# Latent attention and expert layer on one core: TensorE's attention program unrolled, one softmax division moved to the next window, three more units written back to PSUM

## The chip, the cores and the metric

The kernel runs on one core of a Trainium2 chip. The metric is device time in microseconds of one execution. The engines of the core work side by side and meet at semaphores: TensorE (PE) multiplies matrices and writes PSUM, VectorE (DVE) and ScalarE (ACT) work elementwise, GpSimd (POOL) too but without PSUM, and SyncE (SP) issues DMAs, each after the one before it in its program.

## What is computed

Two layers, each added to its input. The first is attention of 1024 tokens of 256 numbers (4 batches, 16 heads of 64) over 1024 + 128 keys, of which 77 come from the context and the rest of that tile is masked. The second is a mixture of 8 experts with a shared one. Only the attention matters for the change:

```python
    qn = rmsnorm(q, qn_g) * scale
    kn = rmsnorm(k, kn_g)
    sim = jnp.einsum('bhid,bhjd->bhij', qn, kn)
    sim = jnp.where(padded_mask[:, None, None, :], sim, max_neg)
    attn = jax.nn.softmax(sim.astype(jnp.float32), axis=-1).astype(sim.dtype)
    out = jnp.einsum('bhij,bhjd->bhid', attn, v)
```

All matrix products are taken in about float32 accuracy by splitting each factor into an upper and a lower part and multiplying three of the four combinations.

## The kernel before

The attention runs as 32 **windows**. A window is one pair of heads of one batch: `Window(v, s)`, with `s` 0 or 1 and `v` from 0 to 15, so that `w = 2 v + s` counts from 0 to 31. Windows with even w and the odd one behind it form a *pair* here; a preparation pass stands ahead of the first (`v = -1`). Every engine runs the same list of windows, its own part of each.

A window has 18 **units** d = 0 to 17. Units 0 to 8 go through the nine key tiles for the first 512 queries of both heads (half 0), units 9 to 17 for the last 512 (half 1). Unit d goes through the engines like this:

- PE `scores(w, d)`, line 972: six products of keys and queries into the bank pair `ps_s[d % 2]`.
- ACT, lines 828 and 829: the exponential once into `pr_hi` (rounded, upper part) and once in full, to `full_of(d)`. For the units in `SPARED` (0, 1, 9, 16, 17) that is the SBUF tile `pr[d % 2]`; for the others the scores in `ps_s` are overwritten with it.
- DVE, line 718: `pr_lo = full - pr_hi`, the lower part, called lo(d) below. It raises `s_lo`.
- PE `values_half` for unit d, line 1008: the first half of the value products is issued in unit d + 2 (`first`), the second in unit d + 3 (`second`), into `ps_o`.

The scores of unit d + 2 go into the bank pair that unit d used. PE therefore waits ahead of `scores(d + 2)` for `s_exp` of unit d (ACT's reading is over) where d is in `SPARED`, and for `s_lo` of unit d (DVE's reading is over too) where it isn't. In the units 2, 4, 6, 8, 11, 13 and 15 PE has further work: it turns keys and queries of the next window (line 902) and projects those of the window after (lines 925, 938). The units 16, 17, 0 and 1 have none.

The value products carry a 65th row, the sum of the exponentials. When the nine tiles of a half are done, DVE copies `ps_o` to `o_sb[h]` (`output`, line 649; in unit 10 for half 0, in unit 1 of the next window for half 1), and PE may not start the next half's values, `first(11)` and `first(2)`, before that copy (`s_o`). The softmax's division is then a chain of its own for each half, which SP drives:

1. `spread` (lines 305, 307): the row of sums goes to HBM and comes back as 128 x 8.
2. DVE `invert`, line 678: reciprocals.
3. `broadcast` (lines 313, 315): the reciprocals go to HBM (4 KB, "put") and come back copied to 64 partitions, 256 KB, into the **one** tile `rec`.
4. DVE `divide`, line 683: `o_sb[h] = o_sb[h] * rec`.
5. `store` (line 321): 256 KB of `o_sb[h]` to HBM.

Half 0 (tile `o_first`) is copied in unit 10, inverted in unit 13 and divided in unit 16 of its own window; half 1 (`o_second`) is copied in unit 1, inverted in unit 5 and divided in unit 9 of the next window. Since `rec` is one tile, half 1 may be broadcast only when the division of half 0 is over.

POOL squares and normalises the projections of the next window (lines 458, 460, 462); DVE sums its squares in units 14, 17 and 2 (`squares`, lines 691 and 693).

`windows()` writes windows 0 and 1 and the last two out, and runs the 28 between them as a loop of 14 rounds, one pair a round, on PE, ACT, DVE and POOL; SP has a similar loop. Each engine's program holds two versions of the attention, behind a test of the input gains (`either`): with running maxima (`general`) and without. The inputs take the one without.

Of the kernel before, what the change touches and what calls it, by code (L numbers as in the profile page):

```python
# [26 lines left out]
WINDOWS = HEADS // 2  # L27
# [51 lines left out]
PROJECTED = {6: (0,), 8: (1, 2), 11: (3, 4), 13: (5, 6), 15: (7, 8)}  # L79
HALVED = (8, 13, 15)  # L80
BETWEEN = (2, 11)
SPARED = (0, 1, 9, 16, 17)
JOBS = TURNS + KT
PREP = [(c, g) for g in range(2) for c in range(C)] + [(c, None) for c in range(C)]
PREPS = len(PREP)
# [70 lines left out]
def attention(nc, carry, Wout, x, ctx_in, mask, ln_x_g, ln_x_b, ln_l_g, ln_l_b, qn_g, kn_g, lnT, Wq, Wkv, maskRow, maskCol, attT, rden, routed, out, Wfc_s, Wfc, w1S, o_second):  # L156

    with ExitStack() as ctx:
# [121 lines left out]
        def _(sp):  # L280
# [20 lines left out]
            def spread(w, g, before):  # L301

                half = w.n(2, g - 2 * before)
                wait_then(s_o, w.n(2, g + 1 - 2 * before))
                sp.dma_start(rden[bass.ds(half, 1)].unsqueeze(0), o_sb[g][DH:DH + 1, :].unsqueeze(1)).then_inc(s_put, 16)
                wait_then(s_put, w.n(64, 32 * g + 16 - 64 * before))
                sp.dma_start(den[:, g, :], rden[bass.ds(half, 1)].rearrange("h (p k) -> p (h k)", p=P)).then_inc(s_den, 16)
# [11 lines left out]
            def store(w, g, before):  # L319
                wait_then(s_norm, w.n(2, g - 2 * before + 1))  # L320
                sp.dma_start(pair_v[g][bass.ds(w.n(1, -before), 1)].rearrange("w d r n -> d (w r) n"),
                             o_sb[g][0:DH, :].rearrange("d (r n) -> d r n", r=2)).then_inc(s_store[g], 16)
# [26 lines left out]
            def window(w):  # L349
# [15 lines left out]
                    load_mask(mask_b, w.other)  # L365
                if w.attend and not w.first:
                    spread(w, 1, 1)
                    broadcast(w, 1, 1)
                if w.proj and not (opening and w.s == 0):
                    wait_then(s_wlo, w.n(1, 3))  # L370
# [3 lines left out]
                if w.attend:  # L374
                    if not w.first:
                        store(w, 1, 1)
                    spread(w, 0, 0)
                    broadcast(w, 0, 0)
                    store(w, 0, 0)
                if closing(w) and w.s == 0:  # L380
                    sp.wait_ge(s_v, w.n(2, 4))
                    sp.wait_ge(s_nrm, w.n(GROUPS, 2 * GROUPS))
# [153 lines left out]
        def _(dve):  # L536
# [168 lines left out]
            def dve_windows(general):  # L705
                def window(w):
                    for d in range(UNITS):
# [12 lines left out]
                        if w.attend and not w.first:  # L720
                            if d == 5:
                                invert(w, 1, 1)
                            if d == 9:
                                divide(w, 1, 1)
                        if w.attend and d == 13:
                            invert(w, 0, 0)
                        if w.attend and d == 16:
                            divide(w, 0, 0)
                        if w.turn:
                            for i in TURNED.get(d, ()):  # L730
# [124 lines left out]
        def _(pe):  # L855
# [156 lines left out]
            def pe_windows(general):  # L1012
# [47 lines left out]
                        if isinstance(w.v, int) and w.v == -1:  # L1060
                            opening(w, d)

                windows(pe, window)
                for d in range(LAG):
                    values(Window(WINDOWS // 2, 0), d - LAG)

# [840 lines left out]
```

## Time and profile before

| | |
|---|---|
| median of 3 runs | 2600.8 us (2599.01 to 2604.87) |
| the profiled execution | 2599.23 us |
| its span, first to last instruction | 2597.4 us |
| PE busy | 2426.4 us, 93% |
| DVE busy | 1811.9 us, 70% |
| ACT busy | 1705.9 us, 66% |
| POOL busy | 1190.5 us, 46% |
| mean granted clock of TensorE | 0.982 |

The attention's windows fill the span from 93 to about 1770 us; behind them come the output projection and the experts. A busy share is an average over stages, and a busy PE is not a PE at its peak: what counts is where PE stands idle and whom it waits for.

### The profile page before, as it was taken

The page shows a single profiled execution, that of the slowest core. Times are in us where ns is not written, and L with a number is a line of the kernel's source. Part 1 is how long each engine was busy: PE and PEld are TensorE (multiplying, and loading weights), DVE is VectorE, ACT ScalarE, POOL GpSimd, SP SyncE. Part 2 cuts the span into 40 slices and gives each one's busy share as a digit, 9 for nine tenths or more (in the row PEclk, how much of TensorE's full clock was granted, in tenths as well). Part 3 has the DMA queues.
Part 4 walks back from the last instruction along what each step waited for, and adds up shares of the span by engine and source line. Part 5 has one row for each costly group of instructions (what it writes and reads, how often), then busy time and mean ns, then how long its engine had stood idle before and what let it go on. Part 6 is the DMA issues. An engine that isn't in the chain of part 4 may idle for free. (4 is left out here: it accounts for less than half of the span.)

```text
span 2597.4 us, 55511 instructions
## 1 busy us (share of the span) xinstructions
PE 2426.4 (93%) x20310; PEld 2014.8 (78%) x20310; DVE 1811.9 (70%) x2452; ACT 1705.9 (66%) x2286; POOL 1190.5 (46%) x783
## 2 busy tenths in 40 slices
PE   4799999999999999999999999997989999999998
PEld 3677677777776777777777777665989999999997
DVE  7667767677667766776667766775876566767775
ACT  2677777888887887777778777783333334444453
POOL 4334433444334433443344433442533526666665
PEclk8899999999999999999999999998999999999999
DMA  6322332233223332233223322246732459999996
GB/s 196 138 81 81 117 107 79 87 115 107 87 79 113 100 96 86 83 118 104 79 87 115 107 87 79 86 119 129 165 92 72 139 176 321 322 319 318 325 321 173
DMA packets 231564, 363.77 MB, mean 140 GB/s; under 512 B 59559, under 2 KB 139739, under 8 KB 227400
## 3 DMA queue, kind: packets, MB, share of 16 engines
q1 hardware_dynamic: 204694, 301.66, 37.7%
q0 software_dynamic: 25696, 58.82, 8.0%
q8 instruction: 164, 2.69, 0.4%
q10 hardware_dynamic: 978, 0.34, 0.1%
q14 instruction: 32, 0.26, 0.0%
HBM read 280.90 MB, written 79.85 MB: 139 GB/s over the span
## 5 line engine op out<-in xcount | busy, mean ns | idle before, releaser
L718 DVE TENSOR_TENSOR pr_lo<-ps_s,pr_hi 128x1024 fp32r<-128x1024 f32 x416 | 505.0, 1220 | 287.0 <-ACT ps_s L829 287.0
L828 ACT ACTIVATE pr_hi<-ps_s 128x1024 fp32r<-128x1024 f32 x512 | 526.2, 1028 | 231.9 <-PE ps_s L972 160.8
L1008 PE MATMUL ps_o<-pr_hi,vA 64*65 64x512 f32 x2292 | 489.7, 399 | 52.5 <-DVE pr_lo L718 31.6
L1008 PE MATMUL ps_o<-pr_lo,vA 64*65 64x512 f32 x2292 | 483.0, 392 | 0.0
L1008 PE MATMUL ps_o<-pr_hi,vC 64*65 64x512 f32 x2292 | 482.1, 391 | 0.0
L460 POOL TENSOR_TENSOR rs<-ss,minus_half 128x16 f32<-128x16 f32 (+1 forms) x96 | 225.7, 2351 | 480.8 <-DVE ss L693 480.8
L1666 ACT ACTIVATE ht<-f_ps_h,b 128x256 f32<-128x256 f32 x440 | 184.6, 471 | 341.6 <-PE f_ps_h L1598 341.6
L829 ACT ACTIVATE ps_s<-ps_s 128x1024 f32<-128x1024 f32 x384 | 392.5, 1022 | 0.0
L458 POOL TENSOR_TENSOR sq<-raw 128x1024 f32<-128x1024 f32 (+1 forms) x96 | 166.2, 1731 | 436.9 <-ACT raw L773 436.9
L1598 PE MATMUL f_ps_h<-xT_hi,w 128*128 128x256 f32 x1760 | 355.4, 285 | 3.6 <-DVE xT_lo L1700 3.1
L718 DVE TENSOR_TENSOR pr_lo<-pr,pr_hi 128x1024 fp32r<-128x1024 f32 x160 | 241.0, 1508 | 159.1 <-ACT pr L829 154.5
L1611 PE MATMUL f_ps_y<-w,h_hi 128*128 128x256 f32 x1760 | 325.8, 283 | 0.0
L1598 PEld LDWEIGHTS f_ps_h<-xT_hi,w 128*128 128x128 f32 x1760 | 288.2, 190 | 4.5 <-DVE xT_lo L1700 3.9
L1008 PEld LDWEIGHTS ps_o<-pr_hi,vA 64*65 64x65 f32 x2292 | 179.8, 133 | 137.9 <-issue 53.3
L1525 POOL TENSOR_TENSOR w<-w2raw,w 128x1024 fp32r<-128x1024 f32 x80 | 206.3, 2580 | 171.9 <-ACT w L1652 168.5
L1611 PEld LDWEIGHTS f_ps_y<-w,h_hi 128*128 128x128 f32 x1760 | 272.4, 190 | 0.0
L972 PE MATMUL ps_s<-q_hi,k_hi 64*128 64x512 f32 x1152 | 241.4, 398 | 28.7 <-issue 20.9
L1611 PE MATMUL f_ps_y<-w,h_lo 128*128 128x256 f32 x880 | 249.0, 283 | 0.0
L1598 PE MATMUL f_ps_h<-xT_lo,w 128*128 128x256 f32 x880 | 248.9, 283 | 0.0
L1008 PEld LDWEIGHTS ps_o<-pr_lo,vA 64*65 64x65 f32 x2292 | 179.0, 133 | 88.7 <-issue 1.6
L938 PE MATMUL ps_m<-w_sb,lnT_sb 64*128 64x384 f32 (+1 forms) x2304 | 241.0, 329 | 3.6 <-DVE k_lo L658 2.5
L972 PE MATMUL ps_s<-q_hi,k_lo 64*128 64x512 f32 x1152 | 238.6, 392 | 0.0
(220 smaller groups left out, 4611.8 us busy)
## 6 DMA issues: line engine op xcount, KB each, us to landing
w<-w1S_dram SPq DMA_DIRECT2D x160, 512.0 KB, 6.0
lnT_sb<-lnT_dram SPq DMA_DIRECT2D x31, 2304.0 KB, 9.6
w2raw<-in_L_ffn_Wproj SPq DMA_DIRECT2D x78, 512.0 KB, 6.8
w1S_dram<-cut POOLq DMA_DIRECT2D x36, 512.0 KB, 3.0
rec<-rden_dram SPq DMA_DIRECT2D x63, 256.0 KB, 3.8
routed_dram<-empty POOLq DMA_DIRECT2D x28, 387.0 KB, 3.6
xt<-routed_dram SPq DMA_DIRECT2D x39, 258.0 KB, 6.6
w_raw<-in_L_xattn_Wkv SPq DMA_DIRECT2D x66, 128.0 KB, 4.0
```

Source lines behind the costliest of these rows:

```text
L458: g.tensor_tensor(sq[:, 0:n_, j0 * DH:], qk, qk, ALU.mult).then_inc(s_sq, 1)
L460: g.tensor_tensor(rs[:, 0:sums], ss[:, 0:sums], minus_half[:, 0:sums], ALU.pow).then_inc(s_pool, 1)
L718: v.tensor_tensor(pr_lo[:, ring(w, d), :], full_of(d), pr_hi[:, ring(w, d), :].bitcast(F32), ALU.subtract).then_inc(s_lo, 1)
L828: act.activation(pr_hi[:, ring(w, d), :], ps_s[:, d % 2, :], ACT.Exp, bias=bias)
L829: act.activation(full_of(d), ps_s[:, d % 2, :], ACT.Exp, bias=bias).then_inc(s_exp, 1)
L938: ins = mm(ps_m[:, tile % 2, lo:3 * PW], lnT_sb[rows, a, c, tile * P:(tile + 1) * P], w_sb[rows, w.slot, b, c, lo:], start=part == 0 and k ...
L972: ins = mm(ps_s[:, d % 2, 512 * h:512 * h + 512], key[rows, w.slot, keys], x[rows, w.slot, cols], start=not general and i == 0, stop=i == 2)
L1008: ins = mm(ps_o[0:DH + 1, h, :], v_[rows, h], p_[rows, 512 * h:512 * h + 512], start=k == 0 and part == 0 and i == 0, stop=k == KT - 1 and ...
L1525: nc.gpsimd.tensor_tensor(w2[:, slot, 2 * h:2 * h + 2, 1], w2raw[:, slot, 2 * h:2 * h + 2], w2[:, slot, 2 * h:2 * h + 2, 0].bitcast(F32), ...
L1598: ins = mm(ps_h[:, p % 2, i, :], w1[:, slot, p, k, lo, i, :], x_[:, parity, k, :], start=k_ == 0, stop=k_ == 3 * C - 1)
L1611: ins = mm(ps_y[:, parity, r, 0:D], h[:, parity, c, r * P:(r + 1) * P], w2[:, slot, p, lo, c % 2, :], start=c == 0 and k_ == 0, stop=c == ...
L1666: ins = act.activation(ht[:, p, i, :], ps_h[:, p % 2, i, :], ACT.Gelu_apprx_tanh, bias=b1[:, slot, p, i:i + 1])
```

## The change

It has three parts, all in the attention.

- TensorE's program for the version without maxima is no longer a loop: all 32 windows are written out. The other engines keep their loops.
- The division of half 0 moves from unit 16 of its window to unit 7 of the next one, two units ahead of the division of half 1; its store moves with it, on SP between the spread and the broadcast of half 1. The last window keeps its division in unit 16.
- `SPARED` shrinks to the units 1 and 9: units 0, 16 and 17 write the full exponential over the scores in PSUM like the others. DVE then reads it from PSUM, and PE waits for DVE, not for ACT alone, ahead of `scores(0)`, `scores(1)` and `scores(2)`.

```diff
-SPARED = (0, 1, 9, 16, 17)
+SPARED = (1, 9)
...
                 if w.attend and not w.first:
                     spread(w, 1, 1)
+                    store(w, 0, 1)
                     broadcast(w, 1, 1)
...
                     spread(w, 0, 0)
                     broadcast(w, 0, 0)
-                    store(w, 0, 0)
+                    if closing(w) and w.s == 1:
+                        store(w, 0, 0)
...
                             if d == 5:
                                 invert(w, 1, 1)
-                            if d == 9:
-                                divide(w, 1, 1)
+                            if d in (7, 9):
+                                divide(w, (d - 7) // 2, 1)
                         if w.attend and d == 13:
                             invert(w, 0, 0)
-                        if w.attend and d == 16:
+                        if closing(w) and w.s == 1 and d == 16:
                             divide(w, 0, 0)
...
-                windows(pe, window)
+                if general:
+                    windows(pe, window)
+                else:
+                    for v in range(-1, WINDOWS // 2):
+                        for s in range(2):
+                            window(Window(v, s))
```

VectorE from unit 16 of window 0 to unit 1 of window 1 (the same stands between any two windows); line 718 is lo(d), lines 691 and 693 are `squares`, line 649 the copy of half 1. Before:

```order
L718 TENSOR_TENSOR pr_lo<-pr,pr_hi 128x1024
L683 TENSOR_TENSOR o_first<-o_first,rec 64x1024
L718 TENSOR_TENSOR pr_lo<-pr,pr_hi 128x1024
L691 TENSOR_REDUCE ss<-sq 128x16
L693 TENSOR_SCALAR ss<-ss 128x16
L718 TENSOR_TENSOR pr_lo<-pr,pr_hi 128x1024
L649 COPY o_second<-ps_o 65x1024
L718 TENSOR_TENSOR pr_lo<-pr,pr_hi 128x1024
```

The same place now, from unit 15 on, where line numbers are two higher:

```order
L720 TENSOR_TENSOR pr_lo<-ps_s,pr_hi 128x1024 x3
L693 TENSOR_REDUCE ss<-sq 128x16
L695 TENSOR_SCALAR ss<-ss 128x16
L720 TENSOR_TENSOR pr_lo<-ps_s,pr_hi 128x1024
L651 COPY o_second<-ps_o 65x1024
L720 TENSOR_TENSOR pr_lo<-pr,pr_hi 128x1024
```

The division of `o_first` is gone from between lo(16) and lo(17), and lo(16), lo(17) and lo(0) read `ps_s`.

VectorE in units 7 to 10 of window 1, before:

```order
L718 TENSOR_TENSOR pr_lo<-ps_s,pr_hi 128x1024 x2
L718 TENSOR_TENSOR pr_lo<-pr,pr_hi 128x1024
L683 TENSOR_TENSOR o_second<-o_second,rec 64x1024
L649 COPY o_first<-ps_o 65x1024
L718 TENSOR_TENSOR pr_lo<-ps_s,pr_hi 128x1024 x4
```

And now:

```order
L720 TENSOR_TENSOR pr_lo<-ps_s,pr_hi 128x1024
L685 TENSOR_TENSOR o_first<-o_first,rec 64x1024
L720 TENSOR_TENSOR pr_lo<-ps_s,pr_hi 128x1024
L720 TENSOR_TENSOR pr_lo<-pr,pr_hi 128x1024
L685 TENSOR_TENSOR o_second<-o_second,rec 64x1024
L651 COPY o_first<-ps_o 65x1024
L720 TENSOR_TENSOR pr_lo<-ps_s,pr_hi 128x1024 x4
```

The division of `o_first` has come in between lo(7) and lo(8); the rest is unmoved.

SyncE in window 28, from the spread of half 1 on. Before:

```order
L305 DMA rden_dram<-o_second 1x1024
L307 DMA den<-rden_dram 128x8
L313 DMA rden_dram<-den 128x8
L315 DMA rec<-rden_dram 64x1024
L290 DMA w_raw<-in_L_xattn_Wq 128x2x128
L290 DMA w_raw<-in_L_xattn_Wkv 128x2x128 x2
L321 DMA attT_dram<-o_second 64x2x512
```

And now:

```order
L305 DMA rden_dram<-o_second 1x1024
L307 DMA den<-rden_dram 128x8
L321 DMA attT_dram<-o_first 64x2x512
L313 DMA rden_dram<-den 128x8
L315 DMA rec<-rden_dram 64x1024
L290 DMA w_raw<-in_L_xattn_Wq 128x2x128
L290 DMA w_raw<-in_L_xattn_Wkv 128x2x128 x2
L321 DMA attT_dram<-o_second 64x2x512
```

The store of `o_first`, with its wait for the division, now stands ahead of the put and of the load of `rec` for half 1.

## Rows read from the trace of the kernel before

**Rows 1.** Waits of all engines, over the span: us in total, times, longest us

```profile
PE ps_o L1008 <- DVE pr_lo L718: 31.6, 18, 3.4
...
PE ps_s L972 <- issue: 20.9, 10, 2.3
...
PE ps_o L1008 <- DVE o_second L649: 16.8, 31, 1.5
```

**Rows 2.** Timeline of PE, window 16 into 17: start us, us, operation, [idle before <-releaser]

```profile
986.45 0.40 PE L972 MATMUL ps_s<-q_hi,k_hi 64*128 64x512 f32 x2
...
996.04 0.45 PE L1008 MATMUL ps_o<-pr_hi,vA 64*65 64x512 f32 x2 [1.66 <-DVE pr_lo L718]
...
1000.53 0.43 PE L972 MATMUL ps_s<-q_hi,k_hi 64*128 64x512 f32 x2
```

**Rows 3.** Timeline of PE, window 17 into 18, where a round ends

```profile
1038.92 0.41 PE L972 MATMUL ps_s<-q_hi,k_hi 64*128 64x512 f32 x2
...
1045.53 0.50 PE L972 MATMUL ps_s<-q_hi,k_hi 64*128 64x512 f32 x2 [2.29 <-issue]
...
1049.78 0.42 PE L972 MATMUL ps_s<-q_hi,k_hi 64*128 64x512 f32 x2
...
1053.55 0.43 PE L972 MATMUL ps_s<-q_hi,k_hi 64*128 64x512 f32 x2
```

**Rows 4.** Timeline of DVE at the same place

```profile
1041.81 2.68 DVE L718 TENSOR_TENSOR pr_lo<-pr,pr_hi 128x1024 fp32r<-128x1024 f32 x1 [2.24 <-ACT pr L829]
1044.42 2.91 DVE L683 TENSOR_TENSOR o_first<-o_first,rec 64x1024 f32<-64x1024 f32 x1
...
1048.39 1.20 DVE L691 TENSOR_REDUCE ss<-sq 128x16 f32<-128x1024 f32 x1
...
1050.15 1.22 DVE L718 TENSOR_TENSOR pr_lo<-pr,pr_hi 128x1024 fp32r<-128x1024 f32 x1 [0.35 <-issue]
```

**Rows 5.** Timeline of POOL, the squaring alone and beside DVE's division

```profile
1025.69 1.89 POOL L458 TENSOR_TENSOR sq<-raw 128x1024 f32<-128x1024 f32 x1 [13.78 <-ACT raw L773]
...
1043.37 2.88 POOL L458 TENSOR_TENSOR sq<-raw 128x1024 f32<-128x1024 f32 x1
```

**Rows 6.** Timeline of ACT, the second exponential of unit 17

```profile
1042.92 1.10 ACT L829 ACTIVATE pr<-ps_s,mcol 128x1024 f32<-128x1024 f32 x1
```

**Rows 7.** Timeline of DVE, units 7 to 11 of window 17

```profile
1014.67 1.23 DVE L718 TENSOR_TENSOR pr_lo<-ps_s,pr_hi 128x1024 fp32r<-128x1024 f32 x1 [1.97 <-ACT ps_s L829]
...
1020.93 1.23 DVE L718 TENSOR_TENSOR pr_lo<-pr,pr_hi 128x1024 fp32r<-128x1024 f32 x1 [2.82 <-ACT pr L829]
1022.07 1.21 DVE L683 TENSOR_TENSOR o_second<-o_second,rec 64x1024 f32<-64x1024 f32 x1
1023.88 1.22 DVE L649 COPY o_first<-ps_o 65x1024 f32<-65x1024 f32 x1 [0.59 <-PE ps_o L1008]
```

**Rows 8.** Timeline of PE, units 7 to 12 of window 17

```profile
1011.80 0.40 PE L972 MATMUL ps_s<-q_hi,k_hi 64*128 64x512 f32 x2
...
1025.98 0.44 PE L1008 MATMUL ps_o<-pr_hi,vA 64*65 64x512 f32 x2
...
1026.72 0.39 PE L972 MATMUL ps_s<-q_hi,k_hi 64*128 64x512 f32 x2
```

**Rows 9.** Timeline of SP's queue, window 17: start us, us of issuing

```profile
1010.30 0.36 SPq L313 DMA_DIRECT2D rden_dram<-den  x1
1011.86 0.54 SPq L315 DMA_DIRECT2D rec<-rden_dram  x1
...
1023.54 0.69 SPq L321 DMA_DIRECT2D attT_dram<-o_second  x1
```

**Rows 10.** Waits of SP's queue, over the span

```profile
SPq L299 <- DMA rden_dram<-o_second: 130.8, 31, 6.2
```

**Rows 11.** Line 315, the load of rec: from its issue to its landing

```profile
DMA to landing us min/median/max: 3.4/3.8/7.4
```

**Rows 12.** Line 321, the store of a divided half, likewise

```profile
DMA to landing us min/median/max: 3.0/3.2/3.5
```

## The prediction

> **What bounds the kernel now.** I read the waits of all engines first. In the attention PE leads and stands idle in few places: 31.6 us in 18 pieces ahead of value products, for a lower part from DVE, 20.9 us in 10 pieces ahead of scores for nothing but "issue", and 16.8 us in 31 pieces for the copy of half 1 [rows 1]. The reader is to see that the counts are those of window boundaries. Then I read PE's timeline over two boundaries. Into an odd window it waits 1.66 us for lo(17), and scores(3) starts 14.08 us after the old window's scores(16) (1000.53 - 986.45) [rows 2]. Into an even window inside the loop it stands 2.29 us with nobody to wait for, and the same stretch takes 14.63 us [rows 3]. That is where PE's round ends, 13 times. Boundaries without such a jump are 18: the 16 into odd windows, and those into windows 2 and 30.
>
> DVE's timeline tells why lo(17) is late [rows 4]: lo(16) takes 2.68 us and the division behind it 2.91, where lo from PSUM takes 1.23 and the same division 1.21 [rows 7]. POOL's squaring, beside that division, takes 2.88 instead of 1.89 [rows 5]. DVE instructions that read two SBUF tiles and POOL's work stretch each other; lo from PSUM doesn't suffer. By the Trainium skill ("SBUF — State Buffer", "Who interferes with whom") the two engines share one pair of ports under an exclusive lock; the durations agree.
>
> **The change, the boundary.** Times from scores(16) = 0, which is 1038.92 [rows 3]. A unit without further work takes PE 2.07: (1049.78 - 1045.53) / 2, less 0.05, since the first product after a halt takes 0.50 and not 0.41 and costs 0.1 once [rows 3].
> - *The jump* goes with the loop. Alone it would be worth little: where PE doesn't jump it waits for lo(17) instead, so 14.63 would become 14.08.
> - *lo(16)* starts at 2.89 as now [rows 4] and ends at 4.12, for it reads PSUM. scores(0) would go at 4.14: no wait to speak of, though it now waits for DVE.
> - *lo(17)*: ACT's second exponential ends at 5.10 (1042.92 + 1.10) [rows 6], with no division ahead of it lo(17) ends at 6.36. scores(1), due at 6.24, goes at 6.41 (0.05 for the wake-up).
> - *lo(0)* stands behind `squares`. POOL's squaring starts at 4.45 and, undisturbed, ends 1.89 later at 6.34 [rows 5]; the sums start at 6.42. From them to lo(0) it is 1.76 now (1048.39 to 1050.15), 0.35 of it idle at DVE's own jump [rows 4]: 1.41 where DVE doesn't jump. lo(0) runs from 7.83 to 9.06, scores(2) goes at 9.11 instead of 8.58. This 0.5 is the price of taking unit 0 out of `SPARED`; the cover that unit 0 had is gone.
> - From scores(2) to scores(3) it is 3.77 as now (1049.78 to 1053.55) [rows 3], the short wait for the copy of half 1 in it; with 0.1 for the restart, scores(3) goes at 12.98.
>
> So 14.08 becomes 12.98, 1.10 less, 18 times; and 14.63 becomes 13.33, since DVE still jumps (0.35), 1.30 less, 13 times. **Gain: 19.8 + 16.9 = 37 us.** ACT's own jump is not seen in the trace; hi(0) has 0.7 before lo(0) would feel it, so I take nothing. From below: if scores(2) need not wait, 0.6 more a boundary, 55 us in all; if ACT and POOL are each 0.4 later, 12 less, 25 us.
>
> **The change, the middle of the window.** Times from scores(7) = 0, which is 1011.80 [rows 8]. The moved division costs DVE nothing by itself: it lies in idle time (1.97 us stand ahead of lo(7) and 2.82 ahead of lo(9) [rows 7]). But `rec` is one tile, and SP issues in order. What was over long before is now a chain:
> 1. lo(7) starts at 2.87, the next DVE instruction 1.14 later as after lo(9) (1020.93 to 1022.07) [rows 7]: the division of half 0 runs from 4.01 to 5.22.
> 2. SP issues the store 0.26 after a division's end (1023.28 to 1023.54) [rows 9]: 5.48.
> 3. The put comes behind it. A put alone lets `rec` be loaded 1.56 after its issue (1010.30 to 1011.86) [rows 9]; one with a long load ahead of it in SP's queue made SP wait 130.8 us in 31 times, 4.2 each and up to 6.2 [rows 10]. So a put is not over before what is ahead of it, and the store takes 3.2 to land [rows 12]: SP goes on at 8.7. The other bound is a put that overtakes: 5.48 + 0.69 of issuing + 1.56 = 7.7.
> 4. `rec` lands 3.8 after its issue, at least 3.4, at most 7.4 [rows 11]. I take the median: 12.5. It came long before the division until now; the division of half 1 started at 10.27 [rows 7].
> 5. DVE stands in order: division 12.5 to 13.7, then the copy of half 0, 13.65 to 14.87 (now from 12.08), then lo(10), 14.8 to 16.03.
> 6. PE: first(11), due at 14.18, waits for the copy until 14.92; scores(12), due at 14.92 [rows 8], waits for lo(10) until 16.08. With 0.1 for the restart PE loses **1.26 us a window**. lo(11) ends at 17.2, before scores(13) wants it at 18.2, so it ends there.
>
> **Cost: 31 x 1.26 = 39 us.** Its bounds: with 7.7 and 3.4 `rec` lands at 11.1 and lo(10) ends at 14.7, inside the cover, cost 0; each 0.1 us that `rec` lands after 11.4 costs 3 us in all, so landing at 13.3 costs 64. I take the store's landing and the median of the load, the rows most like the case.
>
> Here one rule of the notes speaks against the change. What the rows show is in point 3. The Trainium skill ("DMA: Bandwidth & Descriptors", "Queues, rings and completion order") says that a DMA's semaphore increment lands only after every earlier write of the same DMA engine. By that rule the put waits for the store's landing, 8.7 and 39 us; by a put that overtakes it would be 1 us less a window, 8 us in all. The 31 waits of 4.2 us bear the rule out, behind a load and not behind a store.
>
> **Other moves.** The load of the next keys (2.3 MB) no longer stands behind the division and goes out earlier; PE shows no wait for it, so it gains nothing. The `w_raw` loads stand behind the load of `rec` on SP and go 8.6 us later with it (now 1011.86 [rows 9], then 8.7 after 1011.80); they are wanted in unit 16, which starts 27.1 after scores(7) [rows 3, 8]. Writing the full exponential to PSUM I cost at nothing for ACT: it is the same instruction with another target.
>
> **The sum.** 39 - 37 = +2 us on the profiled execution's 2599.2. That execution lies 1.6 below the median of 2600.8; the difference is carried over, so 2603.
>
> **Rivals.**
> - *The put is not held up.* For it: a put's 4 KB are nothing beside the bandwidth, and the long waits of [rows 10] are behind a load ten times the store's size. Against it: the queue is one. `rec` lands at 11.1 to 12.0, cost 0 to 20, net -17 to -37: about 2573.
> - *`rec` comes later still* (the other side). Right behind it SP issues three `w_raw` loads, and POOL's loads are near; landings up to 7.4 occur [rows 11]. It decides from a landing 0.3 after my 12.5; at 4.6 after its issue, 13.3, the cost is 64 and the net +27: 2628. The last two windows, which have no projections between units 7 and 12 to cover anything, go this way as well.
> - *The written-out PE doesn't lose its idle piece*, since its instructions arrive late wherever they come from. For it: "issue" names no releaser. Against it: at the boundaries without a jump, where the code is straight or inside a round, there is no such piece [rows 2]. Then the 13 even boundaries gain nothing: net +19, 2620. The Trainium skill ("Runtime: NRT & Kernel Launch", "Instruction fetch mechanics") says that fetching ahead is sequential and a taken branch breaks it; by that rule the piece goes and this rival is out.
>
> **How the numbers follow.** My case 0.52, from 2588 to 2618 by errors of 0.4 us a window in either term; the first rival 0.22, the second 0.20, the third 0.06. A measurement tells some 0.2%, 5 us, from no change. Of my case I give 0.14 to faster by more, 0.23 to within, 0.15 to slower by more. Faster: 0.14 + 0.22 = 0.36; same 0.23; slower 0.15 + 0.20 + 0.06 = 0.41. The range leaves out the ends of the rivals: 2570 to 2629; my case alone 2588 to 2618.
>
> **What would show it.** In the changed kernel's trace: no idle "issue" piece ahead of scores; scores(16) to scores(3) near 13.0; no 2.9 us division, lo(0), lo(16) and lo(17) at 1.2 us from `ps_s`; a short wait of PE for lo(0) ahead of scores(2). In the middle: DVE idle ahead of the division of `o_second`, ended by the DMA of `rec`, 2.2 us a window; PE idle ahead of first(11) for the copy of `o_first`, 0.7, and ahead of scores(12) for lo(10), 0.4. If DVE doesn't wait for `rec`, the first rival holds; if it waits 3 us or more, the second. The prediction is wrong altogether if windows shorten at the boundary by another amount than they lengthen in the middle and neither chain is in the trace.

## The result

Over four executions each, the changed kernel takes 2626.1 us (2621.1 to 2627.5) and the kernel before 2602.2 (2599.0 to 2604.9). The ratio is 1.0089, with a 95% interval of 1.0073 to 1.0105: **0.9% slower, +24 us**. The forecast was 2603, in a range of 2570 to 2629, so the time lies inside the range, at its far end, beside the second rival (2628) and outside what the prediction gave its own case (2588 to 2618).

The waits of all engines, over the span of the changed kernel (2623.4 us): us in total, times, longest us.

```profile
DVE o_second L685 <- DMA rec<-rden_dram: 87.5, 31, 9.0
...
PE ps_o L1010 <- DVE o_first L651: 52.0, 31, 9.3
...
PE ps_s L974 <- DVE pr_lo L720: 21.7, 33, 7.7
```

"issue" is gone from PE's waits, and so are the 31.6 us for lo(17) [rows 1]. The gain at the boundary is real. In their place DVE waits for `rec` in all 31 windows that divide a half behind it, 2.8 us each on the mean, and PE for the copy of `o_first` that stands behind that division on DVE.

The same place as [rows 3], window 17 into 18, in PE's timeline (start, us, operation, idle before and what ended it):

```profile
1054.03 0.41 PE L974 MATMUL ps_s<-q_hi,k_hi 64*128 64x512 f32 x2
...
1063.47 0.50 PE L974 MATMUL ps_s<-q_hi,k_hi 64*128 64x512 f32 x2 [0.69 <-DVE pr_lo L720]
...
1067.32 0.42 PE L974 MATMUL ps_s<-q_hi,k_hi 64*128 64x512 f32 x2
```

scores(16) to scores(3) is 13.29 us (1067.32 - 1054.03), where it was 14.63. The idle piece of 2.29 us is gone, and a short wait for lo(0) stands ahead of scores(2). DVE there, against [rows 4]:

```profile
1056.92 1.23 DVE L720 TENSOR_TENSOR pr_lo<-ps_s,pr_hi 128x1024 fp32r<-128x1024 f32 x1 [2.24 <-ACT ps_s L831]
1059.14 1.22 DVE L720 TENSOR_TENSOR pr_lo<-ps_s,pr_hi 128x1024 fp32r<-128x1024 f32 x1 [0.99 <-ACT ps_s L831]
1060.41 1.22 DVE L693 TENSOR_REDUCE ss<-sq 128x16 f32<-128x1024 f32 x1
1061.67 0.18 DVE L695 TENSOR_SCALAR ss<-ss 128x16 f32<-128x16 f32 x1
1062.19 1.22 DVE L720 TENSOR_TENSOR pr_lo<-ps_s,pr_hi 128x1024 fp32r<-128x1024 f32 x1 [0.35 <-issue]
```

lo(16), 2.68 us before, takes 1.23, and no division of 2.91 stands behind it. lo(0) stands behind the sums of squares, as forecast.

The middle of window 17, whose scores(7) start at 1025.35. First SP's queue (start, us of issuing), then DVE, then PE:

```profile
1030.80 0.69 SPq L321 DMA_DIRECT2D attT_dram<-o_first  x1
1031.68 0.46 SPq L313 DMA_DIRECT2D rden_dram<-den  x1
1034.35 0.54 SPq L315 DMA_DIRECT2D rec<-rden_dram  x1
```

```profile
1029.36 1.21 DVE L685 TENSOR_TENSOR o_first<-o_first,rec 64x1024 f32<-64x1024 f32 x1
...
1038.18 1.22 DVE L685 TENSOR_TENSOR o_second<-o_second,rec 64x1024 f32<-64x1024 f32 x1 [2.48 <-DMA rec<-rden_dram]
1039.33 1.21 DVE L651 COPY o_first<-ps_o 65x1024 f32<-65x1024 f32 x1
```

```profile
1040.68 0.45 PE L1010 MATMUL ps_o<-pr_hi,vA 64*65 64x512 f32 x2 [1.09 <-DVE o_first L651]
...
1041.72 0.50 PE L974 MATMUL ps_s<-q_hi,k_hi 64*128 64x512 f32 x2
...
1043.90 0.42 PE L974 MATMUL ps_s<-q_hi,k_hi 64*128 64x512 f32 x2
```

Read it as one chain: division at +4.01, store at +5.45, put at +6.33, load of `rec` at +9.00, second division at +12.83, copy, PE's wait of 1.09. scores(7) to scores(13) takes 18.55 us, where it took 16.99 (1028.79 - 1011.80).

The records of the DMA packets show how the put is held. The store's packets (2,048 bytes each) start from 1032.2 to 1033.5, the put's 128 packets of 32 bytes from 1033.4 to 1033.7, so the put's data move only when the store's are nearly through. The last of the store's 16 completions comes at 1034.02, the last of the put's at 1034.19.

By windows, the starts of `scores` in the two traces subtracted from each other:

| us, after less before | sum | of one window |
|---|---|---|
| boundaries into windows 1 to 31 | -41.8 | -1.1 odd, -1.6 even |
| middles of windows 1 to 29, but for 5 and 10 | +41.8 | +1.55 |
| middles of windows 5 and 10 | +12.6 | +6.3 |
| middles of windows 30 and 31 | +13.2 | +10.0, +3.2 |
| window 0, up to its scores(16) | +1.8 | |
| the rest | -1.6 | |
| span | +26.0 | |

So the change wins 42 us at the boundaries, gives all of it back in the regular middles, and loses 26 more in four windows in which `rec` comes later than in the others.

**Windows 5 and 10.** DVE in window 5, whose scores(7) start at 379.80, and SP beside it:

```profile
394.35 2.30 DVE L685 TENSOR_TENSOR o_second<-o_second,rec 64x1024 f32<-64x1024 f32 x1 [4.20 <-DMA rec<-rden_dram]
```

```profile
386.12 0.46 SPq L313 DMA_DIRECT2D rden_dram<-den  x1
390.19 0.53 SPq L315 DMA_DIRECT2D rec<-rden_dram  x1
```

The put takes 4.07 us from its issue to the next DMA, not 2.67. In the records of the DMA packets 120 of its 128 small packets are over by 388.2, and 15 of its 16 completions are there by 388.60, as early as in window 17. A packet of instructions (queue 8, 16,384 bytes) starts at 388.0 and takes 0.947 us; the put's last eight packets run behind it, at 389.0, and the sixteenth completion comes at 390.04, 1.4 us late. That the eight stood behind this packet on one ring is read from the times; the records don't name the ring. The division then starts in the middle of POOL's squaring and takes 2.30, while the squaring is not stretched:

```profile
393.69 1.89 POOL L460 TENSOR_TENSOR sq<-raw 128x1024 f32<-128x1024 f32 x1 [13.63 <-ACT raw L775]
```

PE waits 3.89 instead of 1.09, and what that costs it is more than the wait. The core's work by stretch: us; busy us and instructions of PE, PEld, DVE, ACT, POOL; granted clock; DMA share; GB/s:

```profile
380.00:394.00 14.00, 14.00 (x120) 10.90 (x116) 5.55 (x6) 11.32 (x14) 0.37 (x2) 1.00 0.46 134
394.00:398.00 4.00, 0.11 (x3) 0.10 (x4) 3.65 (x3) 0.49 (x1) 1.57 (x1) 0.76 0.12 29
398.00:403.00 5.00, 5.00 (x24) 3.34 (x26) 2.28 (x3) 1.94 (x2) 0.00 (x0) 0.51 0.25 54
```

After nearly 4 us of idle time PE works for 5 us at a granted clock of 0.51, which is the lower of its two levels (1.2 of 2.4 GHz). From first(11) to scores(13) it takes 5.09 us (403.02 - 397.93), where it took 3.22 in window 17 (1043.90 - 1040.68): another 1.9 us. So the 4.7 us by which this middle is longer than that of window 17 are 1.7 of late landing, 1.1 of stretched division and 1.9 of clock.

**Window 30** has no projections in units 8 to 11, and POOL loads and stores weights there. SP's timeline and DVE's:

```profile
1718.87 0.70 SPq L313 DMA_DIRECT2D rden_dram<-den  x1
1726.02 0.50 SPq L315 DMA_DIRECT2D rec<-rden_dram  x1
```

```profile
1729.77 1.22 DVE L685 TENSOR_TENSOR o_second<-o_second,rec 64x1024 f32<-64x1024 f32 x1 [8.98 <-DMA rec<-rden_dram]
```

The put takes 7.15 us, since the store ahead of it lands only 7.65 after its issue: its packets are mixed with those of POOL's load and store. Some of it is again a packet of instructions. One starts at 1722.7; 120 of the put's packets have started by 1723.9, the last eight start at 1725.3. In e6 the load of `rec` goes at +13.7 as here (+13.6), with such a packet in nearly the same place, in e7 and e12, which have none there, at +11.8 and +11.9. PE stands idle for 9.28 us in this window, and its granted clock is 0.50 for the 5 us behind.

### The profile page after: what moved, and what is told of

It is laid out like the page before. It is cut to its first block and busy times, and to the rows that moved or that the text cites. A ratio compares the mean times of both kernels' runs of the same rounds, so it can differ in the third digit from the quotient of the medians.

```text
span 2623.4 us, 54379 instructions
## 1 busy us (share of the span) xinstructions
PE 2442.9 (93%) x20310; PEld 2018.6 (77%) x20310; DVE 1733.5 (66%) x2452; ACT 1707.0 (65%) x2286; POOL 1161.5 (44%) x783
## 5 line engine op out<-in xcount | busy, mean ns | idle before, releaser
L720 DVE TENSOR_TENSOR pr_lo<-ps_s,pr_hi 128x1024 fp32r<-128x1024 f32 x512 | 621.9, 1219 | 354.3 <-ACT ps_s L831 348.5
L831 ACT ACTIVATE ps_s<-ps_s 128x1024 f32<-128x1024 f32 x448 | 457.1, 1020 | 0.0
L462 POOL TENSOR_TENSOR rs<-ss,minus_half 128x16 f32<-128x16 f32 (+1 forms) x96 | 208.8, 2175 | 523.6 <-DVE ss L695 523.6
L974 PE MATMUL ps_s<-q_hi,k_hi 64*128 64x512 f32 x1152 | 253.2, 417 | 25.3 <-DVE pr_lo L720 21.7
L974 PE MATMUL ps_s<-q_lo,k_hi 64*128 64x512 f32 x1152 | 239.4, 392 | 0.0
```

The costliest lines, as they stand in the source:

```text
L462: g.tensor_tensor(rs[:, 0:sums], ss[:, 0:sums], minus_half[:, 0:sums], ALU.pow).then_inc(s_pool, 1)
L720: v.tensor_tensor(pr_lo[:, ring(w, d), :], full_of(d), pr_hi[:, ring(w, d), :].bitcast(F32), ALU.subtract).then_inc(s_lo, 1)
L831: act.activation(full_of(d), ps_s[:, d % 2, :], ACT.Exp, bias=bias).then_inc(s_exp, 1)
L974: ins = mm(ps_s[:, d % 2, 512 * h:512 * h + 512], key[rows, w.slot, keys], x[rows, w.slot, cols], start=not general and i == 0, stop=i == 2)
```

## The experiments

Theory: the boundary gains as forecast, and the whole loss is the chain on SP, in which the put stands behind the store and `rec` behind the put. Rivals: the loss lies in the division's new place on DVE, in the load of `rec` being slow whoever is ahead of it, or in one of the other two parts. Where a cut below gives `broadcast` a fourth argument, it is called between the put and the load of `rec`.

### TensorE straight and nothing else (e1)

Only the last piece of the diff, on the kernel before.

> The kernel before with one part of the change: TensorE's windows written out. My theory: the piece of 2.29 us ahead of scores(0) goes, and the wait of 1.66 us for lo(17) takes its place at the even boundaries too, so that scores(16) to scores(3) falls from 14.9 on the mean to 14.1 there: some 10 us less in all, 2590. Rival (a written-out TensorE is itself what costs, because its instructions arrive late): idle pieces without a releaser inside the windows, 2610 or more.

Measured: 2588.5 us, ratio 0.9949 (0.9932 to 0.9966). In the median scores(16) to scores(3) is 14.09 into odd windows and 14.44 into even ones, as before (14.09 and 14.45; the 14.63 of [rows 3] is above the median). PE at the latter (window 17 into 18):

```profile
1045.42 0.45 PE L1008 MATMUL ps_o<-pr_hi,vA 64*65 64x512 f32 x2 [1.67 <-DVE pr_lo L718]
...
1049.56 0.44 PE L1008 MATMUL ps_o<-pr_hi,vA 64*65 64x512 f32 x2 [0.80 <-DVE o_second L649]
```

The "issue" piece goes, and PE waits for lo(17) there instead, as at odd boundaries. The third rival (the written-out PE keeps its idle piece) falls. At eight of the 15 even boundaries this gains nothing, at three 0.2 us. The other four, into windows 4, 20, 26 and 28, gain 1.3 to 1.7 each, 6.0 in all. There, in the kernel before, the idle piece of 1.8 to 2.3 us was followed by some 3 us at the lower granted clock (0.66 in the mean of the 5 us from scores(0) on), while the other nine, of 1.7 to 2.3 us, were not; in e1 the granted clock is 1.00 from window 1 to window 30. The trace is 10.7 shorter in all; 2.6 of the rest lie between scores(3) and scores(7) (11.27 in odd windows before, 11.11 now), and their cause was not looked for.

### The division of half 0 back in unit 16 (e2)

```diff
-                            if d in (7, 9):
-                                divide(w, (d - 7) // 2, 1)
+                            if d == 9:
+                                divide(w, 1, 1)
...
-                        if closing(w) and w.s == 1 and d == 16:
+                        if w.attend and d == 16:
                             divide(w, 0, 0)
```

The store goes back with it; TensorE straight and `SPARED = (1, 9)` stay.

> The changed kernel with the division and the store of half 0 put back into unit 16 (TensorE written out, units 0, 16 and 17 still written back to PSUM). My theory: no wait of DVE for rec, units 7 to 13 back at 17.0 us (18.5 in the changed kernel), and the boundary worse than the changed kernel's 12.9, since lo(17) is late by the division again and scores(1) now waits for it: 14.5 to 15.5. In all 2590 to 2610. Rival (the loss comes from the units taken out of SPARED, not from the division's place): as slow as the changed kernel, 2620 or more.

Measured: 2585.7 us, ratio 0.9944 (0.9928 to 0.9961). The middle is back at 16.98 and 17.06, so the moved division, with what hangs on it, is the whole loss of the middle. The boundary is 13.84 and 14.27, that is 1.0 longer than with the division moved, but less than the 14.5 that was expected at least, and the time lies below the expected range as well. DVE in unit 16, and POOL beside it:

```profile
1039.01 1.23 DVE L718 TENSOR_TENSOR pr_lo<-ps_s,pr_hi 128x1024 fp32r<-128x1024 f32 x1 [2.24 <-ACT ps_s L829]
1040.16 1.53 DVE L683 TENSOR_TENSOR o_first<-o_first,rec 64x1024 f32<-64x1024 f32 x1
```

```profile
1038.71 1.90 POOL L462 TENSOR_TENSOR nrm<-raw,rs 128x1024 f32<-128x1024 f32 x1
1040.57 2.88 POOL L458 TENSOR_TENSOR sq<-raw 128x1024 f32<-128x1024 f32 x1
```

The division takes 1.53 us here and 2.91 before. The missing row of the kernel before is POOL's normalisation, ahead of the squaring of [rows 5]:

```profile
1041.51 1.91 POOL L462 TENSOR_TENSOR nrm<-raw,rs 128x1024 f32<-128x1024 f32 x1
```

Now follow the ends. Before, the normalisation ends at 1043.42, lo(16) 1.07 later, the squaring 1.76 behind that (1046.25), the division 1.08 behind that (1047.33). Here the normalisation ends at 1040.61, the division 1.08 later, the squaring 1.76 behind that (1043.45). Alone DVE's piece takes 1.2 and POOL's 1.9. So DVE's work on two SBUF tiles and POOL's take turns, and each waits for what started before it. That also answers a reading of the prediction: the squaring's 2.88 in [rows 5] is a wait for lo(16), not an effect of the division behind it. With lo(16) read from PSUM one turn drops out, and the division is shorter too.

### `rec` loaded ahead of the store (e3)

```diff
                     spread(w, 1, 1)
-                    store(w, 0, 1)
-                    broadcast(w, 1, 1)
+                    broadcast(w, 1, 1, lambda: wait_then(s_norm, w.n(2, -1)))
+                    store(w, 0, 1)
```

The put goes out as soon as half 1 is inverted; between the put and the load of `rec` SP waits for the division of half 0; the store comes last.

> The changed kernel with SP's order altered: the put of half 1 goes out as soon as its reciprocals are there, then SP waits for the division of half 0, issues the load of rec at once, and the store of half 0 behind it. My theory (the chain store, put, load is the whole loss): rec is issued 5.5 us after scores(7) instead of 9.0, lands at 9.5 to 10, ahead of DVE; units 7 to 13 take 17.1 us, the boundary keeps its 12.9 and 13.3; 31 x 1.5 and some 20 us of single late windows go: 2560 to 2568. Rival (the division in unit 7 costs by itself, or the middle is longer for another reason): above 2600.

Measured: 2562.1 us, ratio 0.9853 (0.9836 to 0.9869). SP and DVE in window 17 (its scores(7) start at 991.24):

```profile
989.89 0.36 SPq L313 DMA_DIRECT2D rden_dram<-den  x1
996.75 0.57 SPq L317 DMA_DIRECT2D rec<-rden_dram  x1
997.60 0.69 SPq L323 DMA_DIRECT2D attT_dram<-o_first  x1
```

```profile
1001.51 1.21 DVE L687 TENSOR_TENSOR o_second<-o_second,rec 64x1024 f32<-64x1024 f32 x1
```

The load goes out at +5.5 instead of +9.0, and the second division starts at +10.27, where it stood before the change, without a wait. The middle is 16.98 and 17.06 in all of windows 1 to 29, 5 and 10 among them; window 30 takes 20.35 instead of 25.01. The boundary stays at 12.87 and 13.29. This settles the main point: the place of the two DMAs of the broadcast on SP (the put of 4 KB and the load of `rec`, 256 KB), and not the division's place on DVE, costs the 64 us between 2626 and 2562.

### Which of the two DMAs it is (e4, e8)

In e4 only the put goes out early, and the store stays ahead of the load of `rec`:

```diff
-                    store(w, 0, 1)
-                    broadcast(w, 1, 1)
+                    broadcast(w, 1, 1, lambda: store(w, 0, 1))
```

> As the one before, but the store of half 0 stays ahead of the load of rec; only the put goes out earlier. My theory (the put was held until the store had landed, the load itself is not): rec is issued 6.7 after scores(7), its data run behind the store's in the queue and land at 10.5 to 11.2, the copy of half 0 is late by at most 0.5: 2562 to 2575. Rival (whatever stands behind the store waits for its landing, a load too): rec lands at 12.5 as in the changed kernel, 2615 or more.

Measured: 2563.2 us, ratio 0.9856 (0.984 to 0.9872). In windows 1 to 29 `rec` is loaded at +6.4 and lands 4.2 later, at +10.5, in the median; the middle is 16.98 to 17.09. The load of `rec` behind the store costs next to nothing.

In e8 the put too waits for the division, but goes out ahead of the store; the load of `rec` is behind it:

```diff
-                    store(w, 0, 1)
-                    broadcast(w, 1, 1)
+                    wait_then(s_norm, w.n(2, -1))
+                    broadcast(w, 1, 1, lambda: store(w, 0, 1))
```

> The changed kernel, with the put of half 1 issued after the division of half 0, as in it, but ahead of the store instead of behind it; the load of rec stays behind the store. It separates a put that is late from a put that is held. My theory (the put waits for the store's landing because it stands behind it): rec is issued 1.6 after the put, at 7.1 after scores(7), instead of 9.0, and lands near 11; one run 2562 to 2578. Rival (the put needs 2.6 us at that time wherever it stands): rec is issued at 8.1 or later, 2590 or more.

Measured, in a single execution: 2570.0 us; the middles of windows 1 to 29 are 16.98 to 18.17. SP's queue in one window, where the put starts at 845.04:

```profile
845.04 0.35 SPq L313 DMA_DIRECT2D rden_dram<-den  x1
845.66 0.70 SPq L323 DMA_DIRECT2D attT_dram<-o_first  x1
846.60 0.55 SPq L317 DMA_DIRECT2D rec<-rden_dram  x1
```

From the put to the load it is 1.56 us, as for a put alone [rows 9] (its packets start from 845.9 to 846.1), with a store of 256 KB issued right behind it; with the same store ahead of it, it is 2.67. The put is held by what is ahead of it and not by what follows. Here the Trainium skill ("DMA: Bandwidth & Descriptors", "Queues, rings and completion order": the semaphore increment lands only after every earlier write of the same DMA engine) agrees with the runs: the put is late behind the store and not ahead of it. The packet records add that here the put's data themselves run behind the store's; whether its completion alone would be held, no run separates.

### Unit 0 left in SBUF as well (e5), and all five units (e6)

e5 is e3 with one more edit:

```diff
-SPARED = (1, 9)
+SPARED = (0, 1, 9)
```

> The version with the load of rec ahead of the store (2562 us), and unit 0 back in SPARED (0, 1, 9). My theory: scores(2) no longer waits for lo(0), which stands behind the sums of squares; scores(16) to scores(3) falls from 12.9 and 13.3 to 12.5 at both kinds of boundary, and window 0, where the same wait was 7.7 us, is 2 us shorter: 2545 to 2551. Rival (lo(0) from SBUF is stretched by POOL's work and delays the copy of half 1 as much as the wait did): 2558 to 2566.

Measured: 2532.3 us, ratio 0.9739 (0.9722 to 0.9756), **the fastest version, 2.6% below the kernel before**. The boundary is 12.35 and 12.34: PE no longer waits for lo(0), and DVE's own jump no longer reaches PE. Expected were 12.5 at both kinds of boundary; the gain is 0.5 at odd and 0.9 at even ones, 21.5 us in all. Another 4.8 are between scores(3) and scores(7) (10.99 instead of 11.31 in odd windows), which was not expected and whose cause stays open, and 2.3 in window 0, where 2 were expected. The time lies 13 us below the expected range.

e6 is the changed kernel with `SPARED` as before the change, `(0, 1, 9, 16, 17)`.

> The changed kernel with SPARED as before, (0, 1, 9, 16, 17); written-out TensorE and the moved division stay. It prices the third part of the change. My theory: lo(16) is stretched to 2.7 again and lo(17) to at least 1.5, but scores(0) to scores(2) wait for ACT alone; lo(17) ends near 7 in time for first(1) at 7.6, so the boundary takes 12.4 to 12.8, a little less than the changed kernel's, and the middle stays at 18.5: 2612 to 2624. Rival (reading PSUM in these units is what made the boundary short): boundary 14 or more, 2650 and above.

Measured: 2621.2 us, ratio 1.0077 (1.0058 to 1.0096), 5 us below the changed kernel; the intervals of the two ratios overlap. Its boundary is 12.96 and 13.31, not the 12.4 to 12.8 expected: lo(17) takes 2.91 us in the division's old place, and PE waits 0.5 for it. So the third part of the change is worth nothing as a whole: units 16 and 17 in PSUM save PE's wait for lo(17), and unit 0 in PSUM puts one for lo(0) in its place. Units 16 and 17 in PSUM with unit 0 in SBUF, as in e5, have neither wait.

### TensorE's loop back in the changed kernel (e7), and why it missed

> The changed kernel with TensorE's loop back; the other two parts stay. It prices the first part in the place where it acts. My theory: even boundaries get the idle piece back, now with no wait for lo(17) that it would hide: 13.3 becomes 15.3 at 13 of them, 2646 to 2654. The two windows with a division later than the rest (5 and 10) move or go, since TensorE fetches its instructions at other points. Rival (the piece is hidden behind the waits of the changed kernel): 2624 to 2630.

Measured: 2706.5 us (2695 to 2714), ratio 1.0397 (1.036 to 1.0434), some 55 above the expectation. The boundary into even windows takes 19.4 us. Waits of PE over the span:

```profile
PE ps_s L974 <- issue: 60.0, 13, 5.0
```

Ahead of the 13 scores(0) behind a jump PE is idle for 4.1 to 5.1 us, and not for 2.3 at most. At one of them, from SP's queue and from the table by stretch, with the columns of above:

```profile
1099.00 0.34 SPq L282 DMA_DIRECT2D lnT_sb<-lnT_dram  x1
```

```profile
1100.00:1107.80 7.80, 2.75 (x26) 1.63 (x22) 3.85 (x4) 3.37 (x4) 6.18 (x4) 0.91 0.75 293
1107.80:1113.00 5.20, 5.20 (x24) 3.45 (x26) 1.23 (x1) 1.94 (x2) 3.68 (x3) 0.50 0.02 7
```

The load of the next keys (2.3 MB) is issued 0.6 us behind scores(16) and fills the DMA engines over PE's jump; in the kernel before it stood behind the division on SP and went out some 9 us later, behind the jump. Then PE runs 5.2 us at a granted clock of 0.50. Another expectation held: the late middles moved, to windows 4, 12, 22 and 24. New theory: the instructions behind the jump come by DMA and stand behind this load. Three runs test it.

e10 is the kernel before, with its loop; only the store of half 0 stands behind the load of the keys on SP, not ahead of it, so that the load goes out early.

```diff
                     broadcast(w, 0, 0)
-                    store(w, 0, 0)
+                    if not w.proj:
+                        store(w, 0, 0)
...
                         load_ln(ln_b)
+                    if w.attend:
+                        store(w, 0, 0)
```

> The kernel before, PE's loop, SPARED and both divisions as they were; only on SP, store(w, 0, 0), which waits for the division of half 0 in unit 16, is put behind the lnT load instead of ahead of it, so that the load goes out some 9 us earlier, right behind scores(16) and across PE's jump. Nothing is left out. Theory (the load delays PE's fetch behind the jump): the idle piece ahead of scores(0) of even windows grows from at most 2.3 us to 4 to 5 us, and the clock falls to half for some us behind it, as in the changed kernel with a loop; 14 even boundaries longer by 3 to 5 us each, the time 2645 to 2675. Rival (the jump doesn't care for the load): 2597 to 2606.

Measured: 2646.0 us, ratio 1.0173 (1.0156 to 1.0191). PE at one boundary, then PE's row of waits:

```profile
1074.09 0.79 PE L975 MATMUL ps_s<-q_hi,k_hi 64*128 64x512 f32 x2 [4.31 <-issue]
```

```profile
PE ps_s L975 <- issue: 59.8, 13, 5.1
```

The even boundary takes 18.7 us in the median instead of 14.5. The product of 0.79 us, where one took 0.50 [rows 3], shows the lower clock.

e9 was to hold the load back in e7, until lo(17).

> The changed kernel with PE's loop of 14 rounds put back, as in the run before of that kind, and with one more edit on SP: the load of the keys and inputs (lnT, 2.3 MB) for the window after next waits until DVE has subtracted unit 17 of this window. Open is why PE's jump back, which left it idle for 2.3 us at most in the kernel before, left it idle for 4.2 to 5.1 us in the changed kernel with a loop, followed by 5 us at half the granted clock. Theory: PE's instructions behind the jump are fetched by DMA, and in the changed kernel the lnT load is issued 0.3 us after scores(16) instead of 9.7 us after it, so that it keeps 90% of the DMA engines busy in just these microseconds; the fetch stands behind it, and the long idle time lowers the clock. Then here the idle piece is again 1.7 to 2.4 us, the clock doesn't fall, the even boundary is 14.3 to 15 us instead of 19.45, and the time 2635 to 2655. Rival: the jump is long for another reason that the changed kernel has (the order of the releases, less work queued behind); then the idle pieces stay at 4.2 to 5.1 us and the time near 2700.

Measured: 2720.8 us, and idle pieces of 4.2 to 5.1 us. But the count that SP waited for was one that DVE had reached a window earlier: the load still went out at its early time, and the run only repeats e7. e12 waits for the right one:

```diff
                 if w.proj:
                     wait_then(s_raw, w.n(KT, 3 * KT))
+                    if w.attend:
+                        wait_then(s_lo, w.n(UNITS, UNITS))
```

> The run before it that was to hold the lnT load back waited for a count that DVE had reached a window earlier, so its load still went out 0.3 us behind scores(16), and it only repeated the changed kernel with a loop (2721 and 2707 us). Here SP waits for DVE's subtraction of unit 17 of the same window, some 9 us later, before it loads; PE has its loop of 14 rounds again, the rest is the changed kernel. Theory (PE's fetch behind the jump stands behind the load's packets; the long idle time lowers the clock): the idle piece ahead of scores(0) of even windows is 1.7 to 2.4 us instead of 4.2 to 5.1, no fall of the clock, the even boundary 13.6 to 15 us instead of 19.5, and the time 2630 to 2655. Rival (the load isn't what makes the jump long in the changed kernel): idle pieces of 4.2 to 5.1 us and 2695 to 2725.

Measured: 2656.7 us (2646 to 2665), ratio 1.0211 (1.0173 to 1.0248), 50 us below e7. The same boundary, PE and SP:

```profile
1071.46 0.50 PE L976 MATMUL ps_s<-q_hi,k_hi 64*128 64x512 f32 x2 [1.82 <-issue]
```

```profile
1071.96 0.34 SPq L282 DMA_DIRECT2D lnT_sb<-lnT_dram  x1
```

The idle pieces are 1.7 to 2.3 us again, as in the kernel before. The even boundary is 14.1 to 14.7 at seven jumps; at the other six it is 15.7 to 16.2, with a granted clock of 0.66 in the 5 us behind. These six were not expected, and the time is 2 us above the expected range. The load's time decides the length of the jump, in both directions.

The packet records show the fetch itself. In the kernel before, e7, e9, e10 and e12 two packets of instructions (16,384 bytes) fall between scores(16) and scores(0) at each of the 13 jumps; in e1 and the changed kernel, whose PE is written out while the other engines still jump, there is none at 11 and 12 of these 13 boundaries, and a single one at the rest. The first starts 1.2 to 2.0 us after scores(16) in all five runs. The second starts at 3.4 to 4.0 in the kernel before and e12, and at 5.8 to 6.8 in e7, e9 and e10, and scores(0) follow it by 2.6 to 3.1. So it is the second packet that the load puts off.

The same records bear on windows 5 and 10. Five runs have the changed kernel's order on SP (it, e6, e7, e9, e12). In windows 1 to 29 of them, 17 loads of `rec` go later than +10.3, and each has a packet of instructions that starts between +8.2 and +8.5, while the put runs. Without such a packet none goes later than +9.4. Of 26 other windows with a packet at that time none goes later than +9.4 either, so the packet alone is not enough; that it must fall on the ring with the put's tail is likely but not shown.

So the written-out program is worth about 14 us in the kernel before (e1), and some 80 in the changed one (2706.5 - 2626.1): it is what lets the load go out early at no cost.

### Window 30 (e11)

e5, and window 30 too divides its half 0 in its own unit 16, as window 31 does.

> The fastest version so far (changed kernel; reciprocals put and reloaded ahead of the store; SPARED = 0, 1, 9), and window 30 too divides its half 0 in its own unit 16, as the changed kernel does in window 31 alone. In windows 30 and 31 no projections cover the chain: there scores(7) to scores(13) took 20.2 us in the fastest version instead of 17.1, since the moved division and store hold the reload of rec until the weights' loads are in its way. Expected: 17.0 to 17.5 us there again in window 31 (its first half no longer divides in unit 7) and 30's own piece 17 to 18.5 as the division of window 29 is still moved into it; in all 0 to 3 us less than 2532, 2528 to 2533. Rival: no change in window 30 (it is window 29's division that stands in its unit 7) and a later start of window 31: 2532 to 2536.

Measured: 2531.5 us, ratio 0.9733 (0.9717 to 0.9749), the same as e5. Window 30's middle takes 20.5 (20.2 in e5), as the rival said: what stands in its unit 7 is window 29's division. The time fits both expectations and tells nothing. Window 31's grows from 16.5 to 17.2.

## Why the prediction was right in part

**The boundary: right.** scores(16) to scores(3) is 12.87 into odd windows (12.98 forecast) and 13.29 into even ones (13.33). lo(16), the restart at scores(1), the sums ahead of lo(0) and the wait for lo(0), 0.69 us in the row above, stand where the steps put them. The gain is 42 us and not 37, since four even boundaries of the kernel before took 15.7 to 16.2 us, at the lower clock, and not the 14.63 that was read. One step in it is off: the jump alone would not have made 14.08 of 14.63. e1 has 14.44, since DVE's own jump (0.35 ahead of lo(0) [rows 4]) stays.

**Points 1 and 2 of the middle: right to 0.1** (4.01 and 5.45, forecast 4.01 and 5.48).

**Point 3: right in mechanism, 0.3 short.** The put is held until the store has landed; the store lands at +8.67 (8.7 forecast), but the load of `rec` goes at +9.0, since the put's own completion comes 0.17 behind the store's and SP takes 0.16 more to issue. The first rival, the put that overtakes (+7.7), is out: e8 and e4 show what a put that isn't held would have given.

**Points 4 to 6: the terms add up to 1.55 a window, forecast 1.26.** `rec` is there at +12.8 (forecast 12.5), and PE follows it one to one from there. The forecast's cost of 3 us for each 0.1 us of lateness was sound, its landing was 0.3 too early.

**The step that failed is the last of that part: "Cost: 31 x 1.26".** It priced every window alike. 27 windows cost 42 us (34 by the forecast's price); windows 5, 10, 30 and 31 cost 26 more (5 by that price). The last two were named, in the second rival, without a price of their own; they needed one from the start, since they have no projections as cover. 5 and 10 were not foreseen: a chain without slack takes over every disturbance, here a packet of instructions that runs while the put does, and a PE that stands for 4 us then loses 1.9 more to its clock. Added up: +2 forecast, -5 at the boundaries, +8 in the regular middles, +21 in the four windows, makes the +26 of the traces. That is the second rival's figure (+27), but by fewer and larger delays than it described. That the time lies inside the stated range is luck in part: with those four windows at the price of the others it would be near 2606, inside the forecast's own case; as they are, it is inside only because the range takes in most of the second rival.

**The third part** was counted within the boundary and never by itself. Its cost for unit 0 was named (0.5 a boundary) and accepted; e5 against e3 shows that leaving unit 0 in SBUF was worth 30 us, with e3's order on SP.

**"It gains nothing"**, said of the earlier load of the keys, held only because PE no longer jumps: beside a jump it costs 44 us in the kernel before (e10) and 50 in the changed one (e7 against e12). A moved transfer was checked against PE's waits and not against PE's instruction fetch.

## What to carry to other kernels

When a step moves, write out the order of the DMAs on its queue. In this kernel a 4 KB put that starts a chain belongs ahead of the store of 256 KB: behind it the queue went on 2.67 us after the put's issue, ahead of it 1.56. Price the windows without cover apart from the regular ones, and look for the slack of a chain: where it has none, every chance delay counts, and where it kept TensorE idle for 4 us here, the clock fell too. Before letting a large load go out earlier, ask which engine jumps while it is in flight. And read more than one boundary: the one read here hid four that were 1.1 to 1.5 us longer.

## What the runs showed of the hardware that was not expected

- TensorE's jump at a loop's end leaves it idle for 1.7 to 2.3 us with the DMA engines free (a share of 0.02 and 0.03 over 4.5 us at the jump into window 18, in the kernel before and in e12) and for 4.1 to 5.1 us while a load of 2.3 MB keeps them busy (e7, e10). The Trainium skill ("Runtime: NRT & Kernel Launch", "Instruction fetch mechanics") says that a taken branch whose target is not among the pages of instructions already there waits for a DMA to fetch it; the traces agree, with two packets of instructions at each jump, and add the size and what lengthens it.
- Behind the longer pieces the granted clock is 0.50 for 5 us at 11 of 13 jumps in e7, and 0.51 to 0.66 in the mean of 5 us in e10. It also fell, for some 3 us, behind pieces of 1.8 to 2.3 us: at 4 of 13 jumps of the kernel before and at 6 of 13 of e12. The length of the piece alone doesn't tell the two kinds apart (2.29 without a fall, 1.81 with one).
- One packet of instructions, 0.947 us, put off one of the 16 completions of a put of 4 KB by 1.4 us, and the put is over only with the last.
- VectorE's division and POOL's squaring take turns: the one that starts later ends 1.1 us (division) or 1.8 us (squaring) after the other's end, and the first is not stretched. So the division takes 1.21 us alone, 1.53 where POOL's normalisation has 0.45 to go (e2), and 2.30 where it starts 0.7 behind the squaring, which keeps its 1.89 (window 5 of the changed kernel).
